# Neighbourhood attention: two heads' score matmuls issued together, four score banks and two transpose banks

## The reference, cut to what matters

```python
attn = jnp.einsum('bhijc,bhikjlc->bhijkl', q, k_win)      # 8 heads, 4 numbers a head
attn = attn + bias.transpose(0, 1, 3, 2, 4)[None]
attn = jax.nn.softmax(attn.reshape(B, nh, H, W, K * K), axis=-1)
out = jnp.einsum('bhijkl,bhikjld->bhijd', attn, v_win)    # 32 numbers a head
```

## Time and profile before

| what | value |
|---|---|
| median of 3 runs | 10392.46 us |
| the profiled execution, first to last instruction (span) | 10375.5 us |
| first score matmul of line 390 starts | 451.1 us |
| last one starts | 2475.9 us |
| TensorE busy, whole span | 8825.9 us (85%) |
| VectorE busy | 5783.3 us (56%) |
| ScalarE busy | 4145.5 us (40%) |
| GpSimd busy | 3261.0 us (31%) |

### The profile page before, as it was taken

The page is one execution under the profiler, slowest core; times in us unless marked ns, Lnnn a source line. Parts: engine busy times, 40 slices in busy tenths (PEclk is TensorE's granted clock), DMA queues, the critical chain, the costliest instruction groups (busy, mean ns, idle before and its releaser), DMA issues. The chain is left out here.

```text
span 10375.5 us, 158377 instructions
## 1 busy us (share of the span) xinstructions
PE 8825.9 (85%) x47072; PEld 4663.3 (45%) x47072; DVE 5783.3 (56%) x13683; ACT 4145.5 (40%) x9073; POOL 3261.0 (31%) x1854
## 2 busy tenths in 40 slices
PE   4499989997667999998999989999999885448888
PEld 3355545554444444444444444444444334325555
DVE  4355555555557976675766757766676004324444
ACT  1255555553000055555555555555555660001111
POOL 2000000000000055555555555555555670142211
PEclk8655555555876599999999999999999996569999
DMA  4511121101533001202112021111211004211110
GB/s 137 88 20 20 20 35 20 20 8 49 178 123 103 10 20 28 56 21 56 27 24 56 19 56 30 31 45 30 47 28 41 14 5 127 78 40 42 44 34 21
DMA packets 368839, 480.22 MB, mean 46 GB/s; under 512 B 154040, under 2 KB 322362, under 8 KB 354855
## 3 DMA queue, kind: packets, MB, share of 16 engines
q1 hardware_dynamic: 344551, 426.24, 17.0%
q0 software_dynamic: 23424, 43.45, 1.6%
HBM read 298.80 MB, written 180.34 MB: 46 GB/s over the span
## 5 line engine op out<-in xcount | busy, mean ns | idle before, releaser
L1057 POOL TENSOR_TENSOR a_added<-a_P 128x896 f32<-128x896 f32 x1344 | 2805.3, 2107 | 3517.1 <-ACT a_P L1029 3516.8
L935 DVE TENSOR_REDUCE a_tops<-a_ps 128x1 f32<-128x448 f32 x5600 | 3166.2, 632 | 1322.8 <-PE a_ps L843 1319.5
L1029 ACT ACTIVATE a_P<-a_ps 128x448 f32<-128x448 f32 (+1 forms) x5600 | 2610.3, 548 | 2600.3 <-PE a_ps L901 2599.3
L901 PE MATMUL a_ps<-a_qp,a_kp 98*128 98x448 f32 (+1 forms) x5600 | 1946.8, 399 | 171.4 <-DMA a_qp<-scratch_neg 97.9
L843 PE MATMUL a_ps<-a_hk,a_hq 96*128 96x448 f32 (+1 forms) x4900 | 1922.6, 406 | 118.9 <-DMA a_hk<-scratch_k 96.8
L843 PEld LDWEIGHTS a_ps<-a_hk,a_hq 96*128 96x128 f32 (+1 forms) x4900 | 917.7, 188 | 1205.3 <-DVE a_tops L935 1047.2
L901 PEld LDWEIGHTS a_ps<-a_qp,a_kp 98*128 98x128 f32 (+1 forms) x5600 | 1008.0, 189 | 951.7 <-ACT a_P L1029 637.8
L860 PE MATMUL a_ps<-a_P,a_vt 128*32 128x448 f32 (+1 forms) x11200 | 1362.2, 558 | 0.0
L459 DVE CUSTOM_DVE_ANT_0 n_sm<-n_ps,n_bias 112x448 f32<-112x448 f32 x928 | 578.1, 624 | 850.8 <-PE n_ps L390 850.8
L485 ACT ACTIVATE n_P<-n_sm,n_mx 112x448 f32<-112x448 f32 x928 | 620.2, 668 | 845.4 <-DVE n_mx L459 845.4
L400 PE MATMUL n_ps<-n_idn,n_P 112*112 112x112 f32 x3712 | 923.5, 404 | 21.5 <-DVE n_P L466 21.5
(11 more groups left out here) (174 smaller groups left out, 6476.7 us busy)
## 6 DMA issues: line engine op xcount, KB each, us to landing
a_qp<-scratch_q SPq DMA_DIRECT2D x168, 224.0 KB, 3.8
a_hq<-scratch_q SPq DMA_DIRECT2D x84, 392.0 KB, 7.3
a_hk<-scratch_k SPq DMA_DIRECT2D x84, 392.0 KB, 8.6
a_kp<-scratch_k SPq DMA_DIRECT2D x96, 320.0 KB, 4.9
scratch_t<-o_ts SPq DMA_DIRECT2D x8, 3136.0 KB, 13.2
e_w<-in_w SPq DMA_DIRECT2D x16, 1024.0 KB
p_xs<-in_x SPq DMA_DIRECT2D x4, 3136.0 KB, 15.3
scratch_v<-p_vs SPq DMA_DIRECT2D x4, 3136.0 KB, 12.5
```

The source lines that it names most:

```text
L901: pe.matmul(PS[0:rows_of(t), i_s % 3, 0:GW], kp[0:98, hh, 128 * t:128 * t + rows_of(t)], qp[0:98, hh, GW * j:GW * j + GW], start=True, sto ...
L935: dve.tensor_reduce(tops[0:rows_of(t), KT * hh + t, k:k + 1], PS[0:rows_of(t), MAX + i % MAXES, 0:GW], AX_X, ALU.max).then_inc(topped, 1)
L1029: act.activation(P[0:rows_of(t), (2 * n + pair) % (2 * RING), hh % 2, :], PS[0:rows_of(t), (4 * n + hh) % 3, 0:GW], ACT.Exp).then_inc(expe ...
L1057: pool.tensor_tensor(added2[:, a % 6, :, :], P[:, (2 * n + pair) % (2 * RING), :, :], P[:, (2 * n + 2 + pair) % (2 * RING), :, :], ALU.add ...
```

## The change

Three things change, all in `layer0_attend`. First, TensorE issues the scores in the even steps alone, two at a time: S(n) and S(n + 1), heads 0 and 1 or 2 and 3 of a query tile, which lie in different strips of 32 rows. Second, the score banks are four (0 to 3), chosen by head; the pair waits for the two units four steps back. Third, the transpose banks are two (4 and 5), so T(m) waits for copy(m - 2) where it waited for copy(m - 3). The step offsets, the work of VectorE and ScalarE and their order are as they were.

```diff
-        BS, BT, BO = 0, 3, 6
+        BS, BT, BO = 0, 4, 6
...
-                    if n < U:
+                    if n < U and n % 2 == 0:
                         r, hh = divmod(n, 4)
-                        if n >= 3:
+                        if n >= 4:
                             pe.wait_ge(maxed, it * U + n - 2)
-                        rows = slice(32 * hh, 32 * hh + 16)
-                        pe.matmul(PS[0:TT, BS + n % 3, 0:KW].rearrange("p (c s t) -> p c s t", c=4, s=SUB),
...
+                        for h in (hh, hh + 1):
+                            rows = slice(32 * h, 32 * h + 16)
+                            pe.matmul(PS[0:TT, BS + h, 0:KW].rearrange("p (c s t) -> p c s t", c=4, s=SUB),
...
-                        if m >= 3:
-                            pe.wait_ge(copied, it * U + m - 2)
+                        if m >= 2:
+                            pe.wait_ge(copied, it * U + m - 1)
                         for c in range(4):
-                            last = pe.transpose(PS[0:TT, BT + m % 3, TT * c:TT * c + TT],
+                            last = pe.transpose(PS[0:TT, BT + m % 2, TT * c:TT * c + TT],
...
-                            dve.tensor_tensor_reduce(out=sm[:, n % NSM, :], in0=PS[0:TT, BS + n % 3, 0:KW],
+                            dve.tensor_tensor_reduce(out=sm[:, n % NSM, :], in0=PS[0:TT, BS + n % 4, 0:KW],
...
-                        act.activation(PTs[:, m % NPT, :], PS[0:TT, BT + m % 3, 0:KW], ACT.Copy).then_inc(copied, 1)
+                        act.activation(PTs[:, m % NPT, :], PS[0:TT, BT + m % 2, 0:KW], ACT.Copy).then_inc(copied, 1)
```

More of the change, by code:

```diff
@@ L384, in _ @@
                 for n in range(4 * QT + MIX):
-                    if n < U:
+                    if n < U and n % 2 == 0:
                         r, hh = divmod(n, 4)
-                        if n >= 3:
+                        if n >= 4:
                             pe.wait_ge(maxed, it * U + n - 2)
-                        rows = slice(32 * hh, 32 * hh + 16)
-                        pe.matmul(PS[0:TT, BS + n % 3, 0:KW].rearrange("p (c s t) -> p c s t", c=4, s=SUB),
-                                  qp[rows, TT * r:TT * r + TT],
-                                  kp[rows, :, TR * kv[r]:TR * kv[r] + 56].rearrange("p s (c t) -> p c s t", c=4),
-                                  start=True, stop=True).then_inc(scored, 1)
+                        for h in (hh, hh + 1):
+                            rows = slice(32 * h, 32 * h + 16)
+                            pe.matmul(PS[0:TT, BS + h, 0:KW].rearrange("p (c s t) -> p c s t", c=4, s=SUB),
+                                      qp[rows, TT * r:TT * r + TT],
+                                      kp[rows, :, TR * kv[r]:TR * kv[r] + 56].rearrange("p s (c t) -> p c s t", c=4),
+                                      start=True, stop=True).then_inc(scored, 1)
                     if TURN <= n < U + TURN:
```

## The result

The changed kernel takes 10451.23 us, median of 3 runs (10450.41 to 10460.88), against 10392.46: a ratio of 1.0066 with a 95% interval of 1.0048 to 1.0084. The forecast was 10420 with a range to 10455, so the time lies inside the range, but the loss of 59 us is twice the 28 that were forecast. The profiled execution has a span of 10448.6 us and took 10450.41: only 1.8 us lie around a span. So most of the 17.0 that I added to the span of before was the difference between its profiled execution and the median of its runs, not time outside the span.

The account below looks back on a forecast made before the run. TensorE was taken to bound the kernel; after the change the late copy sets 4.26 us per pair. 3.45 us per pass, 27.6 over eight, made the span 10403.1; with 17.0 added, 10420 us, range 10388 to 10455.

Parts of the forecast that it names:

- the 17.0: Whole time: median of the runs lies 17.0 us above the profiled execution's span, added to 10403.1 to give 10420.
- What bounds the kernel: Mid-pass, before the change: TensorE sets the pace at 1.2 GHz, 2.10 us per unit.
- The second score costs 0.01 us: TensorE, mid-pass: a second score in another strip costs about 0.01 us, so a pair frees 0.63 of 4.20.
- T(n - 3) waits for copy(n - 5) behind exp(n): Odd steps: the transpose waits for ScalarE's late copy, TensorE idles 0.70 us, two units take 4.26 against 4.20.
- The release of 0.05 us: From the end of the releasing work to TensorE's start are 0.05 us, so the odd transpose starts at 2.80.
- The upper bound: Pair's period with a later first score and the longest copy: 4.31 us, sum +48 us (10441).
- The end of a pass: Last score comes with S(114), not 2.10 behind it, so T(112) starts at 6.17, 0.25 us earlier than before.
- The sum: Per pass 0.58 + 3.1 - 0.25 = 3.45 us longer, eight passes 27.6 us.
- The freed time arrives: Rival: transposes don't run into the copy, TensorE's 3.56 sets the pace, 266 us less, near 10125; chance 0.11.
- The pair is slow together: Rival: two strips share what they stream, both scores late, period 4.90, 294 us more, near 10685; chance 0.04.
- The strips don't overlap: Rival: second score runs behind the first, TensorE ready at 2.74, time as forecast; counted within the chain's 0.80.
- The clock rises: Rival: two strips at once bring TensorE to 2.4 GHz in this stage, some 430 us less, 9960; chance 0.02.

Follow-up runs that it names:

- e5: Kernel before (single scores, three and three banks) with ScalarE's copy(n - 5) ahead of exp(n) in a step: 10339.61 us, 1.0000 of before.
- e3: Changed kernel with ScalarE's two instructions of a step exchanged, copy(n - 5) ahead of exp(n): 10109.43 us, 0.9725 of before.
- e1: Kernel before, single scores in three banks, with only the transpose banks cut to a ring of two: 10456.45 us, 1.0059 of before.
- e4: Changed kernel's pairs of scores, but with three score banks and three transpose banks: 10118.42 us, 0.9737 of before.
- e2: Changed kernel with the transpose's two waits swapped, so that `copied` rides on its weight load: 10439.20 us, 1.0040 of before.
- e7: e6 with TensorE's transposes and value products grouped T T M M in every second step, offsets one later: 9572.62 us, 0.9260 of before.
- e6: e3 with all four heads of a query tile scored at once instead of pairs: 9920.46 us, 0.9592 of before.
- e8: e7 with pairs of scores instead of fours: 9948.25 us, 0.9577 of before.

## Why the prediction was half right, step by step

*What bounds the kernel.* Right. TensorE's 2.10 per unit at 1.2 GHz set the pace: ScalarE's order alone changed nothing (e5).

*The second score costs 0.01 us.* Right, in mid-pass too: pairs 3.55 apart in e3 against a sum of 3.56, and fours in 0.72 us.

*T(n - 3) waits for copy(n - 5) behind exp(n).* Right. It is the odd T that waits, for the copy, and e1, e3 and e4 show it from three sides. The pieces 0.90, 0.66, 0.67, 0.52, 0.92 and 0.54 came out within 0.01.

*The release of 0.05 us.* This is the step that failed. I took it from two rows in which the late semaphore rides on the matmul. In T it stands as a wait of its own, and the release takes 0.12: 4.33 and not 4.26 per pair. The upper bound, 4.31, was made of other terms and fell short of it too; that the time still lies in the range is luck, owed to the room that I left above the bounds. It is 3.7 us of 52 pairs in a pass, and another 0.17 in the releases at its start. The trace of before had a case to read, at the end of a pass:

```profile
694.30 0.55 ACT L492 ACTIVATE n_PTs<-n_ps 112x448 f32<-112x448 f32 x1 [0.92 <-PE n_ps L400]
...
694.96 1.19 PEld L413 LDWEIGHTS n_ps<-n_PTs,n_vt 112*32 112x32 f32 x32 [0.20 <-issue]
```

M(112) needs the copy that ends at 694.30 + 0.55 = 694.85, and starts at 694.96, 0.11 behind. There too the trace has the wait for `copied` on an instruction ahead of the weight load. I passed over it. e2 takes the 0.07 away again.

*The end of a pass.* Off by 0.26 against me. I had T(112) 6.17 behind S(114), and it came at 6.43. Step 114 is one of those in which VectorE also reads an output bank (line 431 at 699.54), which pushes line 460 of the last unit to 699.72, and with it the exp and the copy that T(112) waits for. That makes 0.19 of the 0.26; the other 0.07 is once more the release of T, 0.12 behind its copy. I had listed that read-out as harmless in mid-pass, where it is, and forgot it at the end.

*The sum.* 3.45 per pass forecast; 3.45 + 0.17 + 3.7 + 0.26 = 7.6 found, which is 61 us for eight passes beside the 61.6 of the stage. Almost all of what was missing, 3.9 of 4.1 us in a pass, is the release. The offset of 17.0 us happened to bring the forecast nearer to the median than its working deserved.

*The rivals.* The freed time arrives: it didn't, but it is real, and e3 and e4 bring it in (0.9725 and 0.9737; the rival's 10125 is 0.9743 of before). The pair is slow together: no, VectorE starts 0.90 behind. The strips don't overlap: they do. The clock rises: not in the changed kernel; in e7 it did, with another order. The Trainium skill, "TensorE: Matmul & The Clock Gate", Part 3, "The cost: per-tile semaphore tail", says that the increments of tiles that end together serialise. They delayed the first score by nothing that these rows show: VectorE starts 0.90 to 0.91 us behind one, two, three or four scores.

## What to carry to other kernels

When a change takes a buffer from one ring to feed another, walk the chain that frees the smaller ring through every queue it stands in. Here the copy that frees a bank stood behind an exponential that needs the newest score, and one bank fewer tied TensorE to the full length of that chain; exchanging two instructions on ScalarE turned a loss of 59 us into a gain of 287. A chain that now decides must be priced with releases of the same form as its own: the wait that rides on the instruction and the one that stands alone differ by 0.07 us, which over 416 periods was half of the result.

## What the runs showed of the hardware that was not expected

- A semaphore that comes late released TensorE 0.05 us after the end of the copy where the wait rode on the transpose's weight load (e2), 0.11 to 0.12 where it was an instruction of its own (the changed kernel, e1).
- Four matmuls of 16 contraction rows in four strips of 32 rows, into four banks, took 0.72 us where one takes 0.71, at the lower clock (e6).
- TensorE with matmuls in flight for 97% of the first pass before, and for 95% of the whole stage, was granted 0.51: 1.2 GHz, but for a short stretch at the ends of its first seven passes, which begins, in the first of them, while 48 value products follow each other. It stayed there with fours (e6, 0.51) and with T T M M for pairs (e8, 0.51, in flight for 94%). With fours and T T M M together (e7) most of each pass runs at 2.4 GHz (1.00 from 800 to 900 us). TensorE is in flight for less of the time there, 77.4 of 100 us, but that is after the rise, when each matmul is shorter; shortly before it was in flight all the time. By the estimate above the change of level gives some 200 of the 348 us between e6 and e7; what in the order of the matmuls brings it, beyond these kernels, is left open.
